# Single-precision matmuls in the first two stages of a perceiver layer, one per product, with the squares of the raw keys on GpSimd

## What is computed

```python
# _L0_xattn_ref: queries, keys and values of the input come through fp8-rounded activations
q, qx = fp8_linear(ln(x), wq), fp8_linear(ln(x), wqx)         # 16 heads x 128 each
k, v  = fp8_linear(ln(x), wk), fp8_linear(ln(x), wv)          # 8 groups x 128 each
core  = gqa(ln(q), ln(k), v)                                  # softmax over 64 keys
kv_x  = einsum('bsi,oi->bso', cond, w_kv_x)                   # keys and values of the context
xcore = gqa(ln(qx), ln(k_x), v_x)                             # softmax over 1601 keys
y     = fp8_linear(cat(core, xcore) / proj_smooth, wproj)
```

## Time and profile before

| | before |
|---|---|
| time, median of 3 runs | 2800.32 us (2798.15 to 2800.42) |
| profiled execution, its own time | 2799.96 us |
| its span | 2798.2 us |
| TensorE busy | 2278.0 us (81%), 18514 matmuls |
| weight loads busy | 1812.5 us (65%) |
| VectorE busy | 2104.4 us (75%) |
| ScalarE busy | 1554.5 us (56%) |
| GpSimd busy | 1571.4 us (56%) |
| stage 1, stage 2, stage 3 | 0 to about 460 us, to about 2440 us, to the end |

### The profile page before, as it was taken

How to read it: one execution, slowest core, us unless ns; L and a number is a source line. 1 busy time by engine, 2 the same in 40 slices (tenths; PEclk the granted TensorE clock), 3 DMA queues, 4 the chain that set the end, 5 groups by cost and what they waited for, 6 DMA issues and landing times. The chain is left out here.

```text
span 2798.2 us, 50477 instructions
## 1 busy us (share of the span) xinstructions
PE 2278.0 (81%) x18514; PEld 1812.5 (65%) x18514; DVE 2104.4 (75%) x4502; ACT 1554.5 (56%) x3129; POOL 1571.4 (56%) x1619
## 2 busy tenths in 40 slices
PE   2466662699999999999999999999999999855556
PEld 1243441578877877877877877877877878644334
DVE  8888885477787778778787787778778787558763
ACT  4455451566666666666666666666666667411211
POOL 2465655766766766767666766766767655340000
PEclk8687875999999999999999999999999999977778
DMA  2001103110010010110110111010010100073100
GB/s 105 16 29 40 46 23 115 55 38 31 26 50 32 25 44 34 31 44 32 32 38 31 34 43 32 32 44 26 31 52 25 32 9 1 1 271 96 40 12 8
DMA packets 74482, 119.45 MB, mean 43 GB/s; under 512 B 21168, under 2 KB 56576, under 8 KB 73216
## 3 DMA queue, kind: packets, MB, share of 16 engines
q1 hardware_dynamic: 74240, 116.23, 12.3%
HBM read 94.20 MB, written 22.02 MB: 42 GB/s over the span
## 5 line engine op out<-in xcount | busy, mean ns | idle before, releaser
L71 PE MATMUL x_kc<-x_wk,x_ctxT 128*128 128x256 f16 x4992 | 622.8, 274 | 52.8 <-POOL x_ctxT L975 40.0
L997 POOL TENSOR_TENSOR x_kT<-x_kf,x_kT 128x512 f16<-128x512 f32 (+1 forms) x448 | 629.6, 1405 | 37.3
L71 PE MATMUL x_ox<-x_ctxp,x_pt 128*128 128x256 f16 x4992 | 619.0, 273 | 0.0
L995 POOL TENSOR_SCALAR x_kT<-x_kf 128x512 f16<-128x512 f32 (+1 forms) x448 | 288.2, 643 | 583.8 <-ACT x_kf L1067 581.8
L71 PEld LDWEIGHTS x_kc<-x_wk,x_ctxT 128*128 128x128 f16 x4992 | 481.6, 98 | 131.6 <-issue 40.2
L71 PEld LDWEIGHTS x_ox<-x_ctxp,x_pt 128*128 128x128 f16 x4992 | 486.3, 98 | 70.1 <-DVE x_on L1328 14.0
L1055 ACT ACTIVATE x_kraw<-x_kc 128x512 f32<-128x512 f32 (+1 forms) x448 | 254.3, 568 | 426.3 <-PE x_kc L71 214.5
L1263 DVE TENSOR_REDUCE x_ss<-x_sq 128x4 f32<-128x512 f32 (+1 forms) x448 | 283.1, 642 | 230.5 <-ACT x_sq L1059 228.9
L1320 DVE TENSOR_TENSOR x_pt<-x_tp,x_pt 128x512 f16<-128x512 f32 (+1 forms) x512 | 297.4, 584 | 117.5 <-ACT x_pt L1094 113.7
L1067 ACT ACTIVATE x_kf<-x_tp,x_hv 128x512 f32<-128x512 f32 (+1 forms) x448 | 330.7, 755 | 76.5 <-PE x_tp L1146 72.7
L1181 PE MATMUL x_tp<-x_ident,x_pb 128*128 128x128 f32 x1664 | 256.5, 274 | 52.8 <-ACT x_pb L1088 50.6
(11 more groups left out here) (234 smaller groups left out, 3181.5 us busy)
## 6 DMA issues: line engine op xcount, KB each, us to landing
x_stage<-in_ctxT SPq DMA_DIRECT2D x32, 800.5 KB, 4.3
x_stage<-in_ctx SPq DMA_DIRECT2D x16, 896.0 KB, 5.1
x_stage<-in_ctx SPq DMA_DIRECT2D x16, 640.0 KB
scr_q<-a_qxT SPq DMA_DIRECT2D x8, 1024.0 KB, 3.9
x_qs<-scr_q SPq DMA_DIRECT2D x16, 512.0 KB, 5.4
scr_core<-a_catc SPq DMA_DIRECT2D x8, 512.0 KB, 2.6
scr_x<-x_catx SPq DMA_DIRECT2D x8, 512.0 KB, 2.6
f_area<-in_wprojT SPq DMA_DIRECT2D x4, 1024.0 KB, 11.4
```

Of the source, the lines that this page charges most:

```text
L71: last = pe.matmul(out, lhs[i], rhs[j], start=start and n == 0, stop=stop and n == len(parts) - 1)
L995: gp.tensor_scalar(dst[0], src, 1.0, 0.0, ALU.mult, ALU.add).then_inc(khi_ready, 1)
L997: gp.tensor_tensor(dst[1], src, dst[0], ALU.subtract).then_inc(kT_ready, 1)
```

## The change

- All operands of matmuls in stages 1 and 2 (`wp`, `xq`, `qT`, `qxT`, `kT`, `vv`, `pt` of stage 1; `wk`, `wv`, `ctxT`, `ctxp`, `kT`, `pt`, `qs`, `onT` of stage 2) are single precision, and each product is one `pe.matmul`. The query scratch in memory has the same bytes as before.
- All splitting goes: on VectorE `low_weights`, `split_v`, the low parts of `pt` and `onT`, on GpSimd `split_heads`, `convert_piece` and `split_unit`. ScalarE writes turned heads and turned keys straight to where TensorE reads them. The two context layouts are loaded by DMA straight into `ctxT` and `ctxp`; `stage` and `kf` go, and the weights of stage 1 are loaded with no wait between the chunks.
- The squares of the raw keys are taken on GpSimd from `kraw`, no longer on ScalarE from `kc`; TensorE's wait for the bank is now one for the copy alone.
- The scale 256 of the context weights goes.

The core of the diff:

```diff
-        wp = sb("wp", [P, 2, KC, 6144], F16)
+        wp = sb("wp", [P, KC, 6144])
-        xq = sb("xq", [P, 4, KC, T], F16)
+        xq = sb("xq", [P, 4, KC, T])
...
                 for k in range(KC):
-                    last = products(pe, pr[:, proj_bank(T, bank)], [xq[:, m, k, bass.ds(T * P, P)]],
-                                    [wp[:, i, k, bank * 512:(bank + 1) * 512] for i in range(2)],
-                                    k == 0, k == KC - 1, EXACT_LEFT)
+                    last = pe.matmul(pr[:, proj_bank(T, bank)], xq[:, m, k, T * P:(T + 1) * P],
+                                     wp[:, k, bank * 512:(bank + 1) * 512], start=k == 0, stop=k == KC - 1)
...
-                split_v(t)
-                for j in range(4):
-                    v.wait_ge(pthi_ready, t * 4 + j + 1)
-                    v.tensor_tensor(pt[:, 1, 4 * j:4 * j + 4, :].rearrange("p u n -> p (u n)"), tr[:, bank_of(("p", j))],
-                                    pt[:, 0, 4 * j:4 * j + 4, :].rearrange("p u n -> p (u n)"),
-                                    ALU.subtract).then_inc(ptlo_ready, 1)
...
+            def load_rows(b):
+                slot = b % 2
+                src = a["ctx"][b]
+                for lo, hi in ((0, 6), (6, 12)):
+                    sp.dma_start(ctxp[:, slot, lo:hi, :], src[lo * P:hi * P, :].rearrange("(c p) n -> p c n", p=P)
+                                 ).then_inc(ctx_ready[slot], 16)
...
+            def load_features(b):
+                for k in range(KC):
+                    sp.dma_start(ctxT[:, b % 2, k, 0:L], a["ctxT"][b, k * P:(k + 1) * P, :]
+                                 ).then_inc(ctxT_ready[b % 2], 16)
...
+            def square(JK, i):
+                u = JK * KU + i
+                n = len(chunks(i)) * 2
+                gp.wait_ge(kraw_ready, u + 1)
+                if u >= 2:
+                    gp.wait_ge(ss_ready, u - 1)
+                k = kraw[:, 4 * i:4 * i + n, :].rearrange("p n d -> p (n d)")
+                gp.tensor_tensor(sq[:, u % 2, 0:n * D], k, k, ALU.mult).then_inc(sq_ready, 1)
...
-                if not (isinstance(JK, int) and u < 2):
-                    act.wait_ge(ss_ready, u - 1)
-                act.activation(sq[:, (jk * KU + i) % 2, 0:n], src, ACT.Square).then_inc(sq_ready, 1)
...
-                act.activation(kf[:, (jk * KU + i) % 4, 0:n], tp[:, bank, 0:n], ACT.Identity, scale=hv[:, 3:4],
-                               bias=hv[:, 7:8]).then_inc(kf_ready, 1)
+                act.activation(kT[:, jk % 2, :, cs[0] * P:cs[0] * P + n],
+                               tp[:, bank, 0:2 * n].rearrange("p (g n) -> p g n", g=2), ACT.Identity,
+                               scale=hv[:, 3:4], bias=hv[:, 7:8]).then_inc(kT_ready, 1)
...
-                if not (isinstance(JK, int) and u < 1):
-                    pe.wait_ge(sq_ready, u)
+                if u >= 1:
+                    pe.wait_ge(kraw_ready, u)
...
-                        ins = products(pe, kc[:, n * 256:(n + 1) * 256],
-                                       [ctxT[:, slot, p, k, c * P:(c + 1) * P] for p in range(2)],
-                                       [wk[:, p, k, gp_ * 256:(gp_ + 1) * 256] for p in range(2)], k == 0, k == KC - 1)
+                        ins = pe.matmul(kc[:, n * 256:(n + 1) * 256], ctxT[:, slot, k, c * P:(c + 1) * P],
+                                        wk[:, k, gp_ * 256:(gp_ + 1) * 256], start=k == 0, stop=k == KC - 1)
...
-                        ins = products(pe, out, [qs[:, b, p, g * P:(g + 1) * P] for p in range(2)],
-                                       [kT[:, j % 2, p, A_, n * 512:n * 512 + w] for p in range(2)], True, True)
+                        ins = pe.matmul(out, qs[:, b, g * P:(g + 1) * P], kT[:, j % 2, A_, n * 512:n * 512 + w],
+                                        start=True, stop=True)
...
-                        ins = products(pe, ox[:, 0:C], [pt[:, A_, p, c * P:(c + 1) * P] for p in range(2)],
-                                       [ctxp[:, slot, p, c, :] for p in range(2)], c == 0, c == CH - 1)
+                        ins = pe.matmul(ox[:, 0:C], pt[:, A_, c * P:(c + 1) * P], ctxp[:, slot, c, :],
+                                        start=c == 0, stop=c == CH - 1)
...
-        DVE_ORDER = [("norm", 0), ("max", 0), ("oa", -2), ("norm", 1), ("m", 0), ("m", 1), ("ob", -2), ("quant", 0),
-                     ("pt", 0, 0), ("pt", 0, 1), ("quant", 1), ("m", 2), ("pt", 0, 2), ("on", -1), ("pt", 0, 3),
+        DVE_ORDER = [("norm", 0), ("max", 0), ("norm", 1), ("m", 0), ("m", 1), ("ob", -2), ("quant", 0),
+                     ("quant", 1), ("m", 2), ("on", -1), ("quant", 2), ("m", 3), ("max", 1), ("quant", 3), ("m", 4),
```

410 lines of the change are left out of this document (123 added, 287 removed), and 6 rows, old and new, of the table DVE_ORDER.

## The result

The changed kernel takes **3101.76 us** (median of four runs, 3100.82 to 3102.68) against 2800.35 us before: a ratio of 1.1078, with a 95% interval of 1.1059 to 1.1098, 301 us more. 3115 was predicted, in a range of 3075 to 3215. Two parts of the sum differ from what was measured, with opposite signs, so that the small distance of the totals is in part luck; much of this text is about them.

The account below looks back on a forecast made before the run. TensorE was taken to bound stage 2, VectorE stage 1. From 2799.96 us, +320 for stage 2's steps, −10 for its start and +7 for stage 1 gave 3117, stated as 3115 us, range 3075 to 3215.

Parts of the forecast that it names:

- TensorE bounds stage 2, and a product costs 4/3: Stage 2: TensorE sets the step; a 256-column product goes from 0.327 to 0.431 us, being two half-rate records.
- 0.2 us a step: Stage 2 steps: TensorE idle time left after the change, for 1.7 us a step before.
- the wait vanishes: Stage 2 steps: TensorE's wait for the exponential before the first turned probabilities goes, with 0.4 to 1.7 us to spare.
- the chain that I followed: Stage 2, seventh key unit through square, sum, norm, max, sign and exponential: probabilities ready at 10.9 or 12.2 us.
- Bank `kc` released by the copy: Stage 2: the bank's release by the copy alone gains nothing, since a key unit comes only every 5 us.
- Stage 1, "+7": Stage 1 becomes 7 us longer in all, with bounds of −25 and +30.
- the 430 that I had called a sign of being wrong: Stage 1: an end below 430 us, or beyond 490, in the trace after would show the prediction wrong.
- The first term (−12 at the start): Start of stage 1: VectorE's removed `low_weights` takes 21 us, of which 12 come through before the first statistics.
- 7 cold or 3.5 warm: Stage 1 tiles: TensorE's eight projection records, 3.51 us before, take 7 or 3.5 by clock; +2.5 a tile taken.
- B: Stage 2: GpSimd's square makes the chain to the first turn outlast TensorE, 2 us a step, total 3240; chance 0.21.
- C: Stages 1 and 2: a call is one half-rate record, 0.216 us per 256-column product, total about 2490; chance 0.02.
- D: Weight loads of 0.19 us a record don't hide: about 4600 in full, 3265 for a tenth; chance 0.04.

Follow-up runs that it names:

- after_order: The changed kernel with the third context unit of the last group ahead of a step's first turned probabilities in TensorE's order: 3070.37 us.
- before_f32: The kernel before with stage 2's key, score and context products as one single-precision matmul each on constants, all splitting still done: 3155.52 us.
- after_sq_act: The changed kernel with the squares of the raw keys back on ScalarE, TensorE waiting for the square: 3110.04 us.
- before_proj_twice: The kernel before with every projection of stage 1 done twice in half precision, the second overwriting the first: 2816.76 us.
- after_proj_half: The changed kernel with half of the columns of stage 1's projections left out: 3065.84 us.
- before_sq_pool: The kernel before with only the squares moved to GpSimd, taken from the copy in SBUF, TensorE waiting for the copy alone: 3083.64 us.
- after_half: The changed kernel with half of the key products and half of the context products of stage 2 left out: 2549.39 us.
- mixed_order: Stage 2 of the kernel before with two context units earlier in TensorE's order; stage 1 single precision except half-precision projections: 2931.35 us.

## Why the prediction came out right, and where it did not

**TensorE bounds stage 2, and a product costs 4/3: right.** Two records to a call, 0.216 and 0.43 us for a record, 0.11 for the short ones, the clock at 1.00, the counts: each was read from stage 3, and each is in the trace after. The sum of 35.0 us of work is the 35.08 that after_order runs at. That the freed engines bring next to nothing in stage 2 held too: some 18 us beside 347, by before_f32 and the estimate for "ob" there.

**The idle that is left, "0.2 us a step", and "the wait vanishes": mis-sized, and on another chain.** A steady step takes 35.52 us where the sum had 35.2, and of 62 steps one, the first, is short (30.7). That makes 15 of the 22 us by which the steps are over. The other 7 are my account of the end, where the last one and a half steps took 24.7 + 13.1 = 37.9 us and the sum had 30.4. Against after_order the idle time is 0.44 us a step.

What failed is the last link of the chain that I followed, from the sign to TensorE's turn: I took the old 2.27 us, and it is 4.8 (1523.29 to 1528.10). The links ahead of it held. From the end of the seventh key unit (1515.02) the sign took 8.3 us, where my terms make 8.6; TensorE took 12.7 to the first turn, where my terms add up to 12.6, not to the 13.0 that I wrote. With 2.27 at the end there would have been 2.1 us to spare. What I did not look at was ScalarE's list, in which the exponential stands behind the turned keys. That it is not the squares after_sq_act shows, and after_order shows that TensorE's order removes it. Besides, a wait of 0.25 in the table costs 0.42 in distances of starts, since the drain of the last record counts as busy. By the same reading the old step's waits of 1.7 us were worth 29.87 − 27.9 = 2.0, with 29.87 the median step before.

**Bank `kc` released by the copy, "nothing": nearly.** The move of the squares is worth 8 us, more than half of it before the first step.

**Stage 1, "+7": the step that failed.** It was −11.3 − 15.3 = −26.6, just past the lower bound of −25, and VectorE starts stage 2 at 433.4 (460.0 before), close to the 430 that I had called a sign of being wrong. The first term (−12 at the start) held. In the tiles two were wrong. First, I let eight records between the turned probabilities and VectorE's next read cost "7 cold or 3.5 warm" in place of 3.51, and took 2.5 of the 3.5 us between the two. TensorE's timeline after:

```profile
213.20 4.49 PE L454 MATMUL a_pr<-a_wp,a_xq 128*128 128x512 f32 x8
...
220.15 3.60 PE L454 MATMUL a_pr<-a_wp,a_xq 128*128 128x512 f32 x8
```

The second run is at 0.43 a record, the high one of the two levels (2.4 GHz), and so as short as the cold half-precision run of 3.51; the first is mixed. The clock granted from 104 to 400 us went from 0.78 to 0.91. That more load of TensorE's alone raises it is shown by before_proj_twice. How the 36.7 us that the columns still cost divide between clock and length is not settled; no run held the one and changed the other.

Second, and larger, the prediction had no term for what GpSimd's splitting did to VectorE. Five kinds of VectorE instruction in a tile have shorter means after the change: the first addition of the statistics by 1.02 us, two rounding passes by 0.26 and 0.72, the merge by 0.25, the four normalised probabilities by 0.26 each. That is 3.3 us a tile and 26 in eight. Putting back such work on GpSimd, with nobody waiting for it, cost 22 us, and 18 is what after_proj_half has beyond VectorE's removed work. I had seen this contention at the start of stage 2 and priced it there ("about 472 without GpSimd beside it"), but in stage 1 I counted the removed GpSimd work as free, because no engine waited for its results for long. The removed work on VectorE was 31 us in eight tiles, and its wait for ScalarE's high part, 14.6 us, went with it. Against all this stands VectorE's wait for TensorE's outputs, 52 us more; 28 of them are there with short projections already (43.0 us in after_proj_half), where the prediction said only that "a wait of 1.95 stands". Together these make −31 − 15 − 26 + 52 = −20, for −15.3 by the starts. The groups of that line, before and after:

```profile
L663 DVE TENSOR_TENSOR a_yf<-a_tr,a_smooth 128x256 f32<-128x256 f32 x64 | 22.2, 418 | 15.3 <-PE a_tr L71 15.2
```

```profile
L601 DVE TENSOR_TENSOR a_yf<-a_tr,a_smooth 128x256 f32<-128x256 f32 x64 | 24.2, 419 | 70.7 <-PE a_tr L484 67.5
```

**Rivals.** B did not come, and it was further off than the prediction's 0.4 to 1.7 us. In the rows above "norm" ends at 1521.08, just when "max" can start on the scores. But a sign that came 2.7 us later would still be in time for the exponential. With a loaded GpSimd its mechanism takes the kernel over, as before_sq_pool shows. C was excluded by the count of records; after_half, which removes less of TensorE's work than C would, shows that it would have been a gain of about 9%, had it held. (C's step of 25 us was priced with VectorE's old 23 us; in the changed kernel VectorE is busy 909.64/64 = 14.) D did not come: distances are 0.216 in stage 2 as well.

## What to carry to other kernels

Count the records of a call before pricing it, and price a matmul by the distance of starts of the same format elsewhere in the trace: fewer instructions can be more time, and on the engine that bounds the stage nothing else makes up for it. Work that leaves an engine off the path is not free of value: look for instructions of the same kind whose lengths differ, and at what stood beside the long ones. When a wait is left, follow it back through the list of every engine on the way, not only through the data: an instruction whose operands are ready can stand behind one whose are not. Such a way can lead back to the waiting engine's own order, which is then the cheapest to change, and not every move of this kind is a gain, as mixed_order shows.
